# A Perceiver block on one core: first cross attention by pairs of key tiles, norms by chunks, weights a stage ahead, joint maximum ahead of the moments

## The reference

```
for layer 0:  x += cross_attention(layernorm(x), ctx, mask)   # 16 heads of width 8, keys masked
              x += gated_delta_rule(layernorm(x))
              x += mixture_of_experts(layernorm(x))           # 8 experts, routed by token
for layer 1:  x += cross_attention(latents=x, x=ctx)          # Perceiver form: both normalized,
                                                              # keys are the context and the latents
              x += gated_delta_rule(x)                        # another form, with convolutions
              x += attention_over_batches + mixture_of_experts
layernorm(x) = (x - mean) / sqrt(var + 1e-5)
cross_attention: softmax(q k^T * scale + mask) v, then an output projection
```

## Time and profile before

| | us |
|---|---|
| three runs | 3076.8, 3080.7, 3083.5 |
| median | 3080.7 |
| the profiled execution | 3079.4 |
| its span in the trace | 3077.6 |
| PE, DVE, POOL, ACT busy | 2819, 1979, 1906, 1480 |

### The profile page before, as it was taken

How to read it: one execution, slowest core, us unless ns; L and a number is a source line. 1 busy time by engine, 2 the same in 40 slices (tenths; PEclk the granted TensorE clock), 3 DMA queues, 4 the chain that set the end, 5 groups by cost and what they waited for, 6 DMA issues and landing times. The chain is left out here.

```text
span 3077.6 us, 66754 instructions
## 1 busy us (share of the span) xinstructions
PE 2819.4 (92%) x22718; PEld 1618.6 (53%) x22765; DVE 1978.6 (64%) x4504; ACT 1479.6 (48%) x2385; POOL 1906.0 (62%) x1278
## 2 busy tenths in 40 slices
PE   5799999999999978998899999999999997888789
PEld 2355555555555566775344444444444443777356
DVE  5477777777777744114667767767767744776653
ACT  3466666666666522333544444444444434223633
POOL 5487878787878721001488888888888872553500
PEclk8899999999999989998999999999999998999789
DMA  7655555555555210001000000000000000000300
GB/s 184 187 174 193 177 190 181 184 186 179 194 175 188 100 58 1 1 0 39 22 33 21 21 32 21 21 32 21 21 32 21 21 1 9 3 3 2 85 5 10
DMA packets 146463, 233.18 MB, mean 76 GB/s; under 512 B 16787, under 2 KB 85851, under 8 KB 146076
## 3 DMA queue, kind: packets, MB, share of 16 engines
q1 hardware_dynamic: 145180, 228.87, 22.7%
q10 hardware_dynamic: 1152, 2.49, 0.6%
HBM read 147.80 MB, written 83.52 MB: 75 GB/s over the span
## 5 line engine op out<-in xcount | busy, mean ns | idle before, releaser
L444 POOL TENSOR_TENSOR sb_a_acc<-sb_a_acc,sb_a_PT 128x1024 f32<-128x1024 f32 x252 | 596.7, 2368 | 36.6 <-ACT sb_a_PT L522 30.3
L522 ACT ACTIVATE sb_a_PT<-ps_a_SC 128x1024 f32<-128x1024 f32 (+1 forms) x416 | 425.8, 1023 | 315.3 <-PE ps_a_SC L794 291.7
L607 DVE TENSOR_REDUCE sb_a_mx<-ps_a_A 128x1 f32<-128x512 f32 x768 | 506.4, 685 | 97.0 <-PE ps_a_A L771 91.8
L1686 POOL TENSOR_TENSOR sb_a_acc<-sb_a_acc,sb_a_PT 128x512 f32<-128x512 f32 (+2 forms) x384 | 487.5, 1269 | 37.3 <-ACT sb_a_PT L1782 10.9
L1782 ACT ACTIVATE sb_a_PT<-ps_a_SC 128x1024 f32<-128x1024 f32 (+2 forms) x256 | 234.3, 915 | 563.0 <-PE ps_a_SC L2061 329.3
L1875 DVE TENSOR_REDUCE sb_a_mx<-ps_a_A 128x1 f32<-128x512 f32 x384 | 256.5, 679 | 280.1 <-PE ps_a_A L2036 240.1
L2080 PE MATMUL ps_a_PV<-sb_a_PT,sb_a_XN 128*128 128x512 f32 (+2 forms) x896 | 434.3, 601 | 2.2 <-ACT sb_a_PT L1782 0.7
L2061 PE MATMUL ps_a_SC<-sb_a_QX,sb_a_XT 128*128 128x512 f32 (+1 forms) x832 | 396.7, 596 | 0.1
L771 PE MATMUL ps_a_A<-sb_a_KS,sb_a_QS 97*128 97x512 bf16 x768 | 301.9, 394 | 30.6 <-issue 17.7
L794 PE MATMUL ps_a_SC<-sb_a_QS,sb_a_KS 105*128 105x128 bf16 (+1 forms) x3328 | 257.3, 220 | 13.4 <-DVE sb_a_QS L621 13.4
L805 PE MATMUL ps_a_PV<-sb_a_PT,sb_a_V 128*32 128x256 f32 (+1 forms) x3328 | 266.7, 392 | 0.4 <-issue 0.3
(11 more groups left out here) (516 smaller groups left out, 5265.3 us busy)
## 6 DMA issues: line engine op xcount, KB each, us to landing
sb_a_C<-in_ctx_dram SPq DMA_DIRECT2D x64, 768.0 KB
a_KD<-sb_a_K SPq DMA_DIRECT2D x192, 256.0 KB, 4.1
sb_a_KS<-a_KD SPq DMA_DIRECT2D x256, 192.0 KB
a_KD<-sb_a_K SPq DMA_DIRECT2D x192, 144.2 KB, 2.7
sb_a_KS<-a_KD SPq DMA_DIRECT2D x256, 108.2 KB
sb_a_QP<-a_QD ACTq DMA_DIRECT2D x6, 384.0 KB, 14.7
sb_a_up<-in_moe_up_dram SPq DMA_DIRECT2D x1, 2048.0 KB, 7.9
sb_a_dn<-in_moe_dn_dram SPq DMA_DIRECT2D x1, 2048.0 KB, 12.0
```

What stands on the lines that cost most here:

```text
L444: pool.tensor_tensor(acc[:, :], first[:, :], PT[slot(a, j)][:, :], ALU.add).then_inc(s["acc"], 1)
L522: act.activation(PT[slot(a, j)][0:n, :], SC[(a + j) % 2][0:n, :], ACT.Exp).then_inc(s["exp"], 1)
L607: v.tensor_reduce(mx[:, p, c:c + 1], A[u % 2][:, :], AXX, ALU.max).then_inc(s["am"], 1)
L1686: pool.tensor_tensor(acc[a][0:m, :], first, PT[u % 4][0:m, HQ * i:HQ * i + HQ], ALU.add).then_inc(s["acc"], 1)
```

## The change

It has five parts.

- *Turned context.* The host hands over the context also as `ctx_T`, with the width along the partitions, and the first attention's weights transposed. SP loads `CT` from it in one transfer per batch; `turn`, its copies and the buffers `C` and `CR` go. The load of b+4 stands at the end of SP's step and waits for the values of b+2; load(2, 0) stands behind `pieces(1)`. The two halves of the keys are now written and read back one after the other.
- *Steps by pairs.* Groups g of two key tiles take the place of tiles. `top` turns into bank `A0`. DVE does `residue` behind the units of a group, and final and invert at the end. POOL adds seven tiles, PE does the ones matmuls of tiles 3, 6, 10, 11 and 12.
- *Norms by chunks* of four tiles, with four `pow` of 128x4; where named, PE does two chunks, other work, and the other two.
- *Weights a stage ahead*, pre-transposed on the host, for the second attention (loaded in delta0) and the ffn (loaded in delta1).
- *The joint maximum* of the second attention ahead of `moments`.

```
-    COUNT = (0, 2, 2, 2, 2, 3, 3, 3, 3, 3, 3, 0, 0)
+    NG = (NK + 1) // 2
+    COUNT = (4, 5, 5, 5, 7, 0, 0)
+    SUMS = (1, 2, 4, 5, 7, 8, 9)
...
             def load(b, a):
-                wait(sp, s["ct"], 4 * (b - 1))
-                sp.dma_start(C[a][:, :, :], ...)
-                sp.dma_start(CR[a][:, :], ...)
+                wait(sp, s["vp"], 4 * (b - 1))
+                sp.dma_start(CT[a][:, :], d["ctx_T"][dsl(b), :, :].rearrange("o d s -> d (o s)")).then_inc(s[f"ld{a}"], 16)
...
# POOL, step
-                    if 2 <= j < 6 and n2:
-                        third(b + 2, j - 2)
+                    if n2 and j in (4, 5, 8, 9):
+                        third(b + 2, (4, 5, 8, 9).index(j))
...
# DVE, step
-                    final(b - 1)
-                for j in range(1, NK):
-                    if n2 and j < 5:
-                        residue(b + 2, j - 1)
-                    if old and j == 1:
-                        invert(b - 1)
+                for g in range(NG):
                     if n1:
-                        for u in units(j):
+                        for u in units(g):
                             tops(b + 1, u)
+                    if n2 and g < 4:
+                        residue(b + 2, g)
...
# PE, step
+                for g in range(NG):
+                    us = list(units(g)) if n1 else []
...
+                    if g + 1 < NG:
+                        for j in pair(g + 1):
+                            scores(b, a, j)
+                            maxima(1)
+                    elif n1:
+                        for j in pair(0):
+                            scores(b + 1, 1 - a, j)
+                    if n2 and g < 4:
+                        keys(b + 2, a, g)
+                    if n2 and g in (4, 5):
+                        values(b + 2, a, g - 4)
+                    if n1 and g == 5:
+                        top(b + 1)
+                    if g > 0:
+                        maxima(1)
+                    for j in pair(g):
+                        products(b, a, j)
+                    if g == NG - 1:
+                        total(b)
+                    maxima(len(us))
+                    if n2 and g in (5, 6):
+                        values(b + 2, a, g - 3)
...
# norm_vector
+    moments(0)
+    moments(1)
+    scaled(0)
+    moments(2)
+    scaled(1)
+    moments(3)
     if meanwhile is not None:
         meanwhile()
...
+    scaled(2)
+    scaled(3)
...
# norm_pool
+    for c in range(NT // 4):
+        r = k.rstd[:, 4 * c:4 * c + 4]
+        pool.wait_ge(s["mean"], 5 * c + 5)
+        pool.tensor_tensor(r, r, k.half[:, 0:4], ALU.pow).then_inc(s["rstd"], 1)
...
# delta0, SP
+            sp.dma_start(k.x1_WT[:, :, :, :].rearrange("p c j d -> p (c j d)"), d["L1_xattn_WT"]).then_inc(s["ldm"], 16)
+            sp.dma_start(k.x1_Wo[:, :, :], d["L1_xattn_Wout"].rearrange("(j p) d -> p j d", p=P)).then_inc(s["ldm"], 16)
+            sp.dma_start(k.x1_cols[:, :], d["L1_xattn_cols"]).then_inc(s["ldm"], 16)
+            for n in ("gm", "bm", "gl", "bl"):
+                sp.dma_start(k.x1_rows[n][:, :], d["L1_xattn_" + n].partition_broadcast(P)).then_inc(s["ldm"], 16)
...
# second attention, DVE, end of a step
-                    if u == 4 and three:
-                        moments(b + 3, 1 - a)
...
                 if one:
-                    top(b + 1, 1 - a)
+                    top(b + 1)
+                if three:
+                    moments(b + 3, 1 - a)
+                if one:
+                    topped(b + 1, 1 - a)
                 if three:
                     norm(b + 3, 1 - a)
```

More of the change, by code:

```diff
@@ L303, in dsl, with units, pair @@
         return bass.ds(b, 1)
-    def units(j):
-        return range(sum(COUNT[:j]), sum(COUNT[:j + 1]))
+    def units(g):
+        return range(sum(COUNT[:g]), sum(COUNT[:g + 1]))
+    def pair(g):
+        return tuple(j for j in (2 * g, 2 * g + 1) if j < NK)
     def summed(b):
-        return (1, 3, 5, 7, 9) if isinstance(b, int) and b == B - 1 else tuple(range(1, PTILE))
+        return (1, 3, 5, 7, 9) if isinstance(b, int) and b == B - 1 else SUMS
     def slot(a, j):
@@ L377, in step @@
                         spill(b + 2, a, g)
-                    for g in range(2):
                         stack(b + 2, a, g)
+                if n4:
+                    load(b + 4, a)
             load(0, 0)
@@ L394, in _ @@
             pieces(1)
+            load(2, 0)
             for g in range(2):
@@ L553, in _ @@
             for c in range(4):
-                turned(1, 1, c)
-            for c in range(4):
                 keys(1, 1, c)
@@ L662, in step, with early @@
                     expand(b + 2, a)
+                if old:
+                    final(b - 1)
+                    invert(b - 1)
+            def early():
+                for c in range(4):
+                    residue(0, c)
             v.memset(mx[:, :, 4:5], 0.1 * MASKED).then_inc(s["mz"], 1)
-            for c in range(4):
-                residue(0, c)
+            norm_vector(k, v, s["n"], meanwhile=early)
             for h, (lo, hi) in enumerate(SPANS):
@@ L860, in _ @@
             for c in range(4):
-                turn(1, 1, c)
-            for c in range(4):
                 keys(1, 1, c)
@@ L1955, in _ @@
                 tops(0, u)
-            top(0, 0)
+            top(0)
+            topped(0, 0)
             step(0, 0, 0, True, True)
```

357 lines of the change are left out of this document (131 added, 226 removed).

## The result

| | before | after |
|---|---|---|
| median | 3080.6 us | 3514.5 us |
| lowest and highest | 3076.8, 3083.5 | 3511.3, 3522.5 |
| span in the trace | 3077.6 | 3515.8 |

The changed kernel is slower: ratio 1.141, 95% interval 1.139 to 1.144. The forecast, 3055 us with a range to 3086, was wrong, and not by a size alone: the largest loss stands in a part that was booked as a gain.

The account below looks back on a forecast made before the run. PE was taken to carry the first attention, its new step bound by the keys chain through DVE's residue. Terms: +28 + 0 - 11.5 - 12 - 9 - 20 = -24.5, giving 3055 us, range 2995 to 3086.

Parts of the forecast that it names:

- The joint maximum first: Second attention's loop: PE's 1.43 us wait every other step goes; -20 us, bounds -26 and -8.
- Late next is the norm of batch b+3: Second attention: with the maximum first, this norm comes 1 to 2 us later and may push copy_out.
- Rival 4: Second attention: the later norm of b+3 holds PE up by as much, 20 us are gone, 3075 us; chance 0.12.
- The keys chain: First attention: keys wait for DVE's residue, now behind the group's units; step 32.2 us, +28 us, bounds 0 to +47.
- The five distances: First attention's step between starts of keys and values: 4.60, 5.27, 4.82, 4.58 and 12.9 us.
- rival 3: First attention: reloaded key rows land late; with 2 us per step, +60 us and 3115 us in all; chance 0.06.
- The bound on the landing, 14.7: First attention, trace of before: key rows needed 14.7 us behind their first issue; some 14.2 in the new step.
- Norms by chunks: delta0, moe0, delta1, ffn: four short `pow` hide the wait for one; -2.5, -3, -2.5, -3.5, together -11.5 us.
- The second attention's start: Weights loaded a stage ahead let rotate start at about 1446 instead of 1457.81; -12 us, or -8 to -14.
- The ffn: Weights ahead start queries and keys at about 2857 instead of 2866.04: -9 us; -12.5 with its norms.
- rival 2: First attention: idles of 0.5 to 0.8 us per group lower PE's clock; +51 us, 3106 in all; chance 0.06.

Follow-up runs that it names:

- e1: Changed kernel with one part undone: in the second attention moments(b+3) ahead of the last units again; 3141.5 us.
- e2: Kernel before the change with one part alone, the joint maximum ahead of moments(b+3); 3463.1 us.
- e4: Changed kernel with one more wait: in the second attention POOL's gain of a batch waits for DVE's norm of the next one; 3171.9 us.
- e7: e1 with the key rows read back piece by piece, six transfers of 16 partitions instead of eight of 96; 3066.5 us.
- e6: e1 with DVE's residue ahead of a group's last two units in the first attention; 3141.0 us.
- e5: e1 with only four of eight key row transfers per half from batch 2 on, part of the computation left out; 3066.9 us.
- e10: e6 plus key rows by mixed 48- and 16-partition transfers, pieces reordered, and whole norms (one `pow`) in delta0 and delta1; 3395.2 us.

## Why the prediction was wrong

- **The joint maximum first: -20 predicted, some +375 measured.** This is the step that failed. PE's wait of 1.4 us at the maximum did go, as argued. But "Late next is the norm of batch b+3, by 1 to 2 us" costed the moved norm at its old duration. Its place was given as a time, and not as a neighbourhood: its 5.4 us belong to a POOL that had two short sums and then a pause of 2.81 us; without the pause they are 15.7. Rival 4 had the right place ("the norm of b+3, later now, holds PE up") and a price of 20 us, a nineteenth of the true one. e1 and e2 show the part, e4 the mechanism. The trace of before gave a hint: single scalings up to 3.53 us at a median of 0.33, and L1862 at 1.04 us, where the same operation takes 0.17 in the timeline after (L1828), with POOL standing. Both were read past.
- **The keys chain: right, and the rows beside it: wrong.** The five distances were forecast within 0.25 us each, 32.2 against 31.3 in all. So the chain's term was not +28 but about 0, its lower bound. e7, which has that chain and rows in time, has a stage of 1086.6 us, 1.4 less than before. The stage lost 70.5 us by rival 3, which had a chance of 0.06: the next rows' first issue comes at 531.29, 19.7 us into the step that begins at 511.56, and rows need 14.0 us from there (497.60 to 511.56). That is 33.7, and the step is 33.84: the loop over the rows' issue and landing sets it, and not PE's chain by the residue, as e6 shows. The rival gave the rows 14.2 us, a step of 32.2 less an issue at about 18, and that would have done for a landing of 14.0; with a chain of 31.3 and an issue at 19.7 there are 11.6. Why it comes at 19.7 is in part the rows' own doing: SP issues the second half until 519.69 and only then writes the next pieces, from 521.65. In e5, with half the transfers, the first issue comes 15.1 us into the step, in e7 14.3. Of the 2.5 us over 31.3, 1.7 are the waits (41.4 us in 800); in the other 0.8 PE is busy for longer, 30.0 us of a step for 29.2 in e7, at a granted clock of 0.98 for 1.00. That the rival's +60 for the stage, on top of +28, lies near the +79 of e1 is partly luck, since the 28 did not come. The bound on the landing, 14.7, was taken from one step of before, where nobody waited for it, so it could only say that so much was enough. The 14.2 lies below it: the row argued for the rival, and I weighed it as one of many.
- **Norms by chunks: -11.5 predicted.** moe0 gained 2.0 of 3. delta0 lost 2.1 and delta1 0.5: the second `pow` of delta0, behind four short ones at 1.0 us each, is what DVE waits for next, which is 0.8 of the 2.1 us; the rest is open. In delta1 the first scalings wait 1.36 us for their own `pow`. What was missed is that POOL has another late instruction in delta0, and that four short `pow` cost more than one.
- **The second attention's start: -12 predicted, about -9 to -11 measured.** rotate comes 10.6 us sooner; the stage of e1 is 9.1 shorter. Right.
- **The ffn: -12.5 predicted, with its norms.** Queries and keys start 13.9 us behind the stage's start for 19.9 before, in e1 as well: -6 for -9. The whole stage is 8.9 shorter in the changed kernel and 2.7 in e1, with the same code: up to the second norm and from it on, the granted clock was 0.82 and 0.95 there, and 0.79 and 0.93 in e1. The kernel before had 0.79 and 0.95, and so has e10, whose ffn takes 225.4 us. So at the same clock the change is worth 6.0 us there, about half of the 12.5, and the rest of the difference between runs goes with the clock.
- **The clock (rival 2).** It did not fall by the idles of 0.2 us ahead of keys; in e7, where they stay and the wait for rows goes, it is 1.00. Idles of the length that the rival named, 0.5 to 0.8 us ahead of keys, did not come about, so it was not tested at them. The clock fell behind waits of 3 us for rows, and to 0.85 in the second attention, as a consequence.

Without the joint maximum and with rows in time, the change is worth what e7 shows: 14 us less than before, where the forecast without its 20 for the joint maximum would be 4.5. It is more because the +28 did not come, and not by 28 because the norms and the weights ahead gave less.
